# Gram products of 128 weight columns split into pairs of 64

## The reference, cut to what matters

```python
xf = x.reshape(B, C, P)                              # 32, 64, 2304
xn = xf / jnp.maximum(jnp.sqrt(jnp.sum(xf * xf, axis=1)), EPS)[:, None, :]
s = jax.nn.relu(jnp.einsum('bcp,bcq->bpq', xn, xn)) ** 2
g = jnp.einsum('oc,bcp->bop', Wc, xf) + bc[None, :, None]
out = jnp.einsum('bpq,bcq->bcp', s, g)
```

## Time and profile before

| what | value |
|---|---|
| median of 3 runs | 5337.25 us (5335.33 to 5337.66) |
| span of the profiled execution | 5332.3 us |
| PE busy | 3735.5 us, 70% of the span |
| DVE busy | 3969.2 us, 74% |
| ACT busy | 3397.9 us, 64% |
| POOL busy | 2944.3 us, 55% |
| chain that ended last | PE 36%, DVE 26%, ACT 5%, DMA 5% |

### The profile page before, as it was taken

How to read it: one execution, slowest core, us unless ns; L and a number is a source line. 1 busy time by engine, 2 the same in 40 slices (tenths; PEclk the granted TensorE clock), 3 DMA queues, 4 the chain that set the end, 5 groups by cost and what they waited for, 6 DMA issues and landing times.

```text
span 5332.3 us, 61957 instructions
## 1 busy us (share of the span) xinstructions
PE 3735.5 (70%) x18367; PEld 1259.1 (24%) x18367; DVE 3969.2 (74%) x5512; ACT 3397.9 (64%) x4285; POOL 2944.3 (55%) x2937
## 2 busy tenths in 40 slices
PE   4888988400599999999999999996000017787888
PEld 1223333200233333333333333332000002222222
DVE  8998988997666666666666654554999947787877
ACT  4777988401676767676676776775566536666665
POOL 6000000058777777777777777774666147666661
PEclk9899999755799999999999999998555558888889
DMA  6100100002112122222212222223555526999997
GB/s 259 33 20 25 29 20 17 15 14 82 28 41 58 40 61 48 47 58 46 62 42 52 52 46 56 42 46 87 189 184 186 184 75 137 150 160 162 158 161 141
DMA packets 332447, 441.38 MB, mean 83 GB/s; under 512 B 183193, under 2 KB 261916, under 8 KB 331500
## 3 DMA queue, kind: packets, MB, share of 16 engines
q1 hardware_dynamic: 209744, 288.12, 19.8%
q0 software_dynamic: 105536, 148.61, 16.0%
q10 hardware_dynamic: 16896, 1.18, 0.2%
HBM read 252.35 MB, written 166.47 MB: 79 GB/s over the span
## 4 chain that ended last, share of the span: by engine, by line
PE 36%; DVE 26%; issue 6%; ACT 5%; DMA 5%; POOL 1%; SPq 1%; DVEq 0%; ACTq 0%; POOLq 0%
PE acc L1830 13%; PE gram L1874 8%; PE gram L1875 6%; DVE s L2404 3%; DMA gs<-gates_d 3%; PE ye L1928 2%; PE up L1940 2%; ACT rel L2064 2%; DVE S L2503 2%; DVE AD L2488 2%; DVE AE L2482 2%; DVE ms L2623 1%; POOL R L1761 1%; PE misc L1804 1%; PE misc L1777 1%
## 5 line engine op out<-in xcount | busy, mean ns | idle before, releaser
L980 POOL DMA_INDIRECT rows<-htab_d,idx x2048 | 2141.5, 1046 | 730.7 <-issue 599.0
L2404 DVE SCALAR_TENSOR_TENSOR s<-gram,rel 128x1024 f32<-128x1024 f32 (+1 forms) x720 | 802.6, 1117 | 849.2 <-ACT rel L2064 844.1
L2064 ACT ACTIVATE rel<-gram 128x1024 f32<-128x1024 f32 (+1 forms) x1080 | 1009.5, 940 | 605.4 <-PE gram L1875 570.4
L1830 PE MATMUL acc<-s,gT 128*64 128x512 f32 (+1 forms) x4320 | 1076.6, 577 | 0.0
L1874 PE MATMUL gram<-hl 128*128 128x512 f16 (+1 forms) x2160 | 776.7, 365 | 117.3 <-DVE s L2404 95.9
L1875 PE MATMUL gram<-hl,lh 128*128 128x512 f16 (+1 forms) x2160 | 765.8, 360 | 0.0
L1761 POOL DMA_INDIRECT R<-seg_d,nidx x576 | 584.5, 1015 | 191.2 <-issue 165.9
L1928 PE MATMUL ye<-hid,w 128*64 128x384 f32 x1536 | 381.4, 577 | 250.8 <-DVE ms L2623 188.5
L1080 POOL IOTA slots<- 64x2048 int32 x1 | 1.8, 1832 | 974.4 <-POOLq L192 974.4
L2156 ACT ACTIVATE hid<-up,b1t 128x768 f32<-128x768 f32 x384 | 333.2, 899 | 259.6 <-PE up L1940 258.4
L1911 PE MATMUL tailsT<-ident,tails 128*20 128x128 f32 x24 | 4.7, 385 | 599.6 <-DVE tails L2511 599.6
(11 more groups left out here) (372 smaller groups left out, 5351.0 us busy)
## 6 DMA issues: line engine op xcount, KB each, us to landing
gs<-gates_d SPq DMA_DIRECT2D x64, 1024.0 KB
rows<-htab_d,idx POOLq DMA_INDIRECT x2048
seg_d<-state SPq DMA_DIRECT2D x32, 996.0 KB, 4.8
raw_d<-w_zeros POOLq DMA_DIRECT2D x48, 512.0 KB, 23.3
raw_d<-rows POOLq DMA_DIRECT2D x32, 768.0 KB, 3.7
tne<-tn_d SPq DMA_DIRECT2D x32, 576.0 KB
x2e<-x_d SPq DMA_DIRECT2D x32, 576.0 KB
out<-res SPq DMA_DIRECT2D x64, 256.0 KB
```

Of the source, the lines that this page charges most:

```text
L980: pool.indirect_dma_start(out=n.rows[:, k % 2, j, :], out_offset=None, in_=n.htabx, in_offset=bass.IndirectOffsetOnAxis(ap=n.idx[:, g % 2, ...
L1830: last = pe.matmul(acc[(par + c) % 2][j * C:(j + 1) * C, 0:w], gT[:, par, 2 * k + j, :], s2[:, u % SLOTS, j * w:(j + 1) * w], start=k == 0 ...
L2064: act.activation(rel[:, t % RELS, 0:2 * w].rearrange("p (j x) -> p j x", j=2), gram[(par + t) % 2][:, :, 0:w], ACT.Relu, scale=1.0 / SPLIT ...
L2404: dve.scalar_tensor_tensor(halves(s2[:, t % SLOTS, 0:2 * w]), gram[(par + t) % 2][:, :, 0:w], 1.0 / SPLIT ** 2, halves(rel[:, t % RELS, 0: ...
```

## The change

Each of the two products of a `j` becomes two of 64 weight columns: the first 64 pixels go to partitions 0 to 63 of the bank, the other 64 to partitions 64 to 127, which are the two column halves of the array that the value products use. The order is `hl` first half, `hl` second half, `lh` first half, `lh` second half. The same numbers are summed in the same places. A gram group has 8 matmuls and 8 weight loads in place of 4 and 4. Nothing else is changed: the banks, the waits and the other engines' programs are as before, and so are the gram products of `weave`.

```diff
                     bank = gram[(par + t) % 2]
                     for j in (0, 1):
-                        pixels = slice((2 * k + j) * P, (2 * k + j + 1) * P)
-                        pe.matmul(bank[:, j, 0:w], hl[:, par, pixels], hl[:, par, o:o + w], start=True, stop=False)
-                        last = pe.matmul(bank[:, j, 0:w], lh[:, par, pixels], hl[:, par, o:o + w], start=False, stop=True)
+                        for own_words, word in ((True, hl), (False, lh)):
+                            for h in (0, 1):
+                                first_pixel = (2 * k + j) * P + h * C
+                                last = pe.matmul(bank[h * C:(h + 1) * C, j, 0:w], word[:, par, first_pixel:first_pixel + C], hl[:, par, o:o + w],
+                                                 start=own_words, stop=not own_words)
                     last.then_inc(pe_gram, 1)
```

## The result

The changed kernel takes 5281.64 us (median of 4 runs, 5276.95 to 5291.28) against 5336.29 for the kernel before in the same session: a ratio of 0.9898, 95% interval 0.9884 to 0.9912, so 54.7 us saved where 59 were forecast. The profiled execution of the changed kernel is the longest of the four: 5291.28 us, with a span of 5289.5. Its span is 42.8 us shorter than the span before. Lines behind 1875 are two higher than before (2064 is now 2066, 2404 is 2406, 2108 is 2110).

The account below looks back on a forecast made before the run. PE bound the image loop, losing time at layout crossings; the chain let 64 us through, POOL about 60, so 59 was taken: span 5332.3 - 59 = 5273, plus 4.95 gives 5278 us, range 5264 to 5326.

Parts of the forecast that it names:

- The crossings: On PE, between gram and value products: both layout changes vanish, saving 0.26 us in each of 45 steps per image.
- The 0.1 us charged for each crossing from transposes to a gram group: On PE, `tokens` and `turn` transposes now change layout before a gram group: 4 x 0.1 us added per image.
- The halves overlap, loads hidden: In PE's gram group: 64-column pairs stream side by side in 0.216 us; loads hidden except 0.06 us after a wait.
- The first rival: In gram groups: exposed loads or short chunks cost more, so the loop gives only 15 to 44 us, 5293 to 5322; chance 0.22.
- The chain: Through a gram bank by PE, ACT and DVE: three steps take at least 5.49 us, limiting what PE's saving yields.
- The working: Image loop's 45 steps worked forward from PE, ACT and DVE durations: 2.68 us saved per image, 64 over 24.
- The three lines of the working: Per image, three groups of steps: 2.37 us saved, 0.89 us saved, and 0.58 us lost again.
- One sign: In the changed profile's image loop: plain steps in triples of about 5.5 us, steps 0 to 2 still 5.5.
- The cap by POOL, about 60: At the loop's end: POOL's gathers ahead let the scan start only about 60 us earlier (54 to 68).
- The scan's start: After the loop: with marks early, the gathered `nb` rows come last, and the first `AE` is at about 3660.
- "The scan follows unchanged": After the image loop: the scan and the experts' layer take as long as before.

Follow-up runs that it names:

- e2_mixed: Changed kernel with j = 0 products again 128 columns wide, only j = 1 split into halves; 5343.11 us, ratio 1.0003 to the kernel before.
- e4_release: Changed kernel with DVE's product from the relu alone and PE waiting only for ACT's relu two steps back; 5413.22 us, ratio 1.0138 to before.
- e3_ahead: Changed kernel with 28 x 64 gathers ahead of the scan instead of 29 x 64, pieces of ten instead of eight; 5329.36 us.
- e9_fewer: Changed kernel with 108 of POOL's 1856 gathers ahead of the scan left out; 5277.98 us, ratio 0.9898 to the kernel before.
- e13_ahead24: Changed kernel with 24 of the gathers ahead of the scan moved into it; 5301.82 us, ratio 0.9934 to the kernel before.
- e7_unroll: Changed kernel with four images in each turn of the first loop instead of two; 5281.38 us, ratio 0.9885 to the kernel before.
- e11_unroll_fewer: Changed kernel with four images per loop turn and 108 gathers ahead of the scan left out; 5256.48 us, ratio 0.9863 to before.
- e1_order: Changed kernel with all four gram products of the first column half before those of the second; 5301.40 us, ratio 0.9923 to before.
- e8_operand: Changed kernel with DVE's product reading ACT's SBUF result twice, PE's wait for the gram bank unchanged; 5424.20 us, ratio 1.0162 to before.
- e10_release_fewer: Changed kernel with DVE's product from the relu alone, gram bank freed early, and 108 gathers left out; 5275.43 us, ratio 0.9898 to before.

## Why the prediction was nearly right

- **The crossings.** Shown: 0.31 before the values became 0.22, and `e2_mixed` brought back the 0.31 and the whole time with it. The 0.1 us charged for each crossing from transposes to a gram group shows as well (0.21 for 0.12).
- **The halves overlap, loads hidden.** Shown by pairs 0.22 us apart. The first rival's loads are 111 ns, not 135, and 0.02 us shows, not 0.06 or more.
- **The chain.** The working gave 2.68 us per image; an undisturbed image gained 2.98, 71 us over 24 where the term said 64. The three lines of the working came out one by one, by the same medians: 2.42 us for 2.37 in the first, 0.98 for 0.89 in the second, minus 0.41 for minus 0.58 in the third. This is more than the right total: the places where PE's gain is let through, and the places where it is lost again (steps 30 to 32, minus 0.47 for minus 0.46), are those forecast. `e4_release` shows that it is the chain: with DVE's product out of it an image loses 4 us more. One sign did not show: steps 0 to 2 take 5.51 us as forecast, but no triple of plain steps comes down to 5.5; the shortest, 12 to 14, went from 5.94 to 5.71.
- **Turn starts: the term that was not in the sum.** The working took each image as undisturbed. All the starts of turns together lost 22 us more than before (a longer stall, and in the first of the two loops a second one of about 2 us inside the first group). The loop's end is therefore 50.7 us earlier in the profile, in place of 64 or more. That profile lies at the low end: with the same loop, `e3_ahead`, `e9_fewer` and `e13_ahead24` end it 53 to 57 us earlier than before. `e7_unroll` shows that the stall is the turn's.
- **The cap by POOL, about 60.** It was not what decided. With two images in a turn the loop ends at about the same time as POOL (`e9_fewer` gains nothing that can be told). Nor was its size right in this profile: POOL's last gather ahead starts 11.0 us later than before (3657.35 for 3646.34), where the prediction left 2. The first `nb` followed at 3659.86; with the 8 us that lay between `nb` and `AE` in `e7_unroll`, its rows were there at about 3668, an estimate, 53 us earlier than before. In `e7_unroll` the last gather is only 0.6 us later than before, so the 11 us do not come with every denser loop; their cause is open. POOL does decide where the loop ends earlier: `e7_unroll` saves 61.6 us against its runs of before, and 78.0 with the gathers thinned out (`e11_unroll_fewer`).
- **The scan's start.** I had the rows of `nb` as the last to come, `AE` at about 3660. In the changed kernel the marks still came last, 21.0 us behind the loop's end (3650.15 to 3671.16), `AE` at 3672.00. So it was the loop's end that set the start of the scan, by way of the marks. In `e7_unroll`, where the loop is done earlier, it is as I wrote: `AE` waits for `nb` and starts at 3657.3.
- **"The scan follows unchanged"** failed a little. The scan alone takes 570.4 to 570.7 us in `before`, `e1_order`, `e2_mixed`, `e9_fewer` and `e11_unroll_fewer`, and 574.3 to 575.6 in the changed kernel, `e4_release`, `e8_operand`, `e7_unroll` and `e10_release_fewer`. In the second group POOL reaches `got` 8 us or more behind the loop's end, and ACT waits some 25 us for `nb` later in the scan; in the first POOL waits for the loop (in `e1_order` it is 3.4 us late), and ACT has no such wait. So a POOL that arrives late stays late for a while, at 4 to 5 us. What is left of the differences in "the rest" lies behind the scan, where the runs spread from 1038 to 1051 us whether POOL was late or not (1046.5 in `e2_mixed`, where it had waited 60.6 us); what moves that part is open.

So 59 stood for 54.7. The loop's own gain was put 7 us too low, the 22 us of the turns' starts were not seen, and the loop, not POOL, set the pace at the end. The forecast stood on POOL's 60. That the loop, 64 + 7 - 22 = 49 us by these terms and 51 to 57 in the profiles, comes out near that figure is luck; that the crossings, the overlap and the chain came out is not.

## What to carry to other kernels

Products of two column layouts that take turns on PE pay at each change of layout; give the wider ones the layout of the others, if two halves side by side stream as fast as one whole, and look for the price as the gap between the last product of one and the first of the other. Before a gain is multiplied by the number of images, look at the images where a turn of the loop starts: more instructions per turn can cost there what they save elsewhere. And when the engine that sets the pace gets faster, the engine beside it, POOL here, is the next to be costed; a trick that loads it (two SBUF operands on DVE) can take back more than the whole gain.

## What the runs showed of the hardware that was not expected

- Products in the two column halves overlap even when four of one half stand ahead of the other's in the program (`e1_order`, group still 0.86 us). The Trainium skill, TensorE: Matmul & The Clock Gate, The mechanism, has matmuls start in strict program order; the starts of `e1_order` do not.
- At a turn's start PE stood 2.94 us, and then 1.84 us more inside its first gram group, for nothing that the profile shows. None stands at a turn entered from the code ahead of the loop. Of the two instruction queues one moved 152 packets before, 187 after and 179 with four images in a turn, the other 119, 119 and 135; that the stalls are code arriving is argued from this, not shown.
- A DVE product with both operands in SBUF runs no slower (1226 ns for 1223) but takes POOL's gathers from 995 to 1089 ns on average, and those that start while it runs from 950 to 1248 ns.
